# Bias projection of an attention block: one product of 512 tokens, or four of 128 tokens in TensorE's column groups

## The reference

```python
v  = (xn @ v_w + v_b)                                  # 16 heads of 16
qm = (xn @ qmod_w + qmod_b)   # [tokens, 16 heads]     the query's bias per head
km = (xn @ kmod_w + kmod_b)   # [tokens, 16 heads]     the key's bias per head
qc, kc = xn @ cq_w, xn @ ck_w                          # 16 heads of 8
scores = kernel[i - j] + qm[i] + km[j] + 0.15 * qc[i] @ kc[j] / sqrt(8)   # causal
attn = softmax(scores); out = LN(h + FFN(h)), h = LN(xn + attn @ v @ out_w + out_b)
gate = silu(FP4-quantised gated FFN of xn);  y = x + out * gate
```

## Time and profile before

| | |
|---|---|
| median of 3 runs | 1970.54 us (1969.98 to 1972.34) |
| profiled execution | 1971.34 us, of which the span of the trace 1969.5 us |
| mean granted TensorE clock | 0.98 of full |
| TensorE (PE) busy | 93% of the span |
| DVE / POOL / ACT busy | 81% / 56% / 46% |
| DMA | mean 84 GB/s |

### The profile page before, as it was taken

The page is one execution under the profiler, slowest core; times in us unless marked ns, Lnnn a source line. Parts: engine busy times, 40 slices in busy tenths (PEclk is TensorE's granted clock), DMA queues, the critical chain, the costliest instruction groups (busy, mean ns, idle before and its releaser), DMA issues.

```text
span 1969.5 us, 41524 instructions
## 1 busy us (share of the span) xinstructions
PE 1841.2 (93%) x12508; PEld 1309.0 (66%) x12508; DVE 1598.7 (81%) x5214; ACT 900.4 (46%) x1816; POOL 1102.8 (56%) x788
## 2 busy tenths in 40 slices
PE   9578899999999999999999999999999999999986
PEld 3134667676776767676776767676676767677765
DVE  6969978888888978888887978888897888888762
ACT  1115454454535454454645554453645444453532
POOL 3424747464655746564665746565664746465471
PEclk9769999999999999999999999999999999999998
DMA  4523223232322323232223323232222322232110
GB/s 138 174 93 89 63 75 117 73 88 69 105 64 82 88 73 106 73 95 73 85 64 99 89 73 106 62 95 83 76 74 73 116 73 88 70 106 67 40 65 22
DMA packets 129154, 165.44 MB, mean 84 GB/s; under 512 B 9821, under 2 KB 90718, under 8 KB 129028
## 3 DMA queue, kind: packets, MB, share of 16 engines
q1 hardware_dynamic: 129034, 164.29, 28.6%
HBM read 127.85 MB, written 36.41 MB: 83 GB/s over the span
## 4 chain that ended last, share of the span: by engine, by line
PE 59%; DVE 20%; issue 14%; ACT 3%; DMA 1%; DVEq 1%; POOL 1%; SPq 1%; ACTq 0%; POOLq 0%
PE ps L738 11%; PE ps L729 11%; PE ps L679 8%; PE ps L696 4%; PE ps L579 4%; PE ps L602 3%; PE ps L636 3%; DVE nmax L994 3%; PE ps L711 3%; PE ps L589 3%; PE ps L652 2%; PE ps L632 2%; DVE ps L994 2%; DVE st L916 2%; DVE slot L1061 1%
## 5 line engine op out<-in xcount | busy, mean ns | idle before, releaser
L1132 POOL TENSOR_TENSOR Pr<-Pr,Tz 128x768 f32<-128x768 f32 (+2 forms) x384 | 477.9, 1273 | 243.7 <-ACT Pr L802 242.7
L994 DVE CUSTOM_DVE_ANT_0 ps<-ps,future 128x512 f32<-128x512 f32 (+3 forms) x1024 | 474.9, 517 | 52.7 <-issue 52.4
L802 ACT ACTIVATE Pr<-ps 128x384 f32<-128x384 f32 x512 | 243.0, 489 | 370.0 <-PE ps L636 367.1
L729 PE MATMUL ps<-catT,w 128*128 128x256 f32 x1024 | 237.3, 380 | 0.7 <-ACT catT L867 0.7
L602 PE MATMUL ps<-KS,QS 108*128 108x512 bf16 (+3 forms) x1024 | 217.2, 303 | 21.0 <-DVE nmax L994 14.7
L738 PE MATMUL ps<-w,gT 128*128 128x256 f32 x1024 | 233.0, 381 | 0.9 <-ACT gT L878 0.9
L791 ACT ACTIVATE ps<-ps 128x512 f32<-128x512 f32 x256 | 150.5, 588 | 132.4 <-PE ps L632 130.2
L1024 DVE SCALAR_TENSOR_TENSOR Pr<-ps,Tz 128x512 f32<-128x512 f32 x256 | 175.0, 684 | 41.3 <-ACT ps L791 37.9
L738 PEld LDWEIGHTS ps<-w,gT 128*128 128x128 f32 x1024 | 190.9, 190 | 25.8 <-ACT gT L878 1.3
L729 PEld LDWEIGHTS ps<-catT,w 128*128 128x128 f32 x1024 | 189.7, 190 | 26.7 <-ACT catT L867 1.0
L696 PE MATMUL ps<-wdT,hqT 128*128 128x256 f32 x768 | 178.2, 381 | 0.7 <-ACT hqT L843 0.7
(11 more groups left out here) (213 smaller groups left out, 3247.9 us busy)
## 6 DMA issues: line engine op xcount, KB each, us to landing
Tz<-kernel_rows SPq DMA_DIRECT2D x128, 512.0 KB, 3.8
KS<-k_parts SPq DMA_DIRECT2D x32, 384.0 KB
QS<-q_parts SPq DMA_DIRECT2D x64, 192.0 KB
hY<-in_x SPq DMA_DIRECT2D x20, 512.0 KB, 4.8
xn<-in_x SPq DMA_DIRECT2D x16, 512.0 KB, 3.6
out<-y SPq DMA_DIRECT2D x16, 512.0 KB, 3.0
q_parts<-q_sp SPq DMA_DIRECT2D x16, 384.0 KB, 3.3
k_parts<-k_sp SPq DMA_DIRECT2D x16, 384.0 KB, 2.4
```

Source lines behind the costliest of these rows:

```text
L729: ins = mm(dst[:, i * n:(i + 1) * n], w1[:, c, f * P:(f + 1) * P], catT[:, c, hf * n:(hf + 1) * n], start=c == 0, stop=c == KD - 1)
L802: inc(af(Pr[:, p % 4, e, at:at + wd], src[:, 0:wd], ACT.Exp), "a_exp")
L994: ins = v.tensor_tensor_reduce(o, o, future[:, S - n:S], -1.0, 3e38, ALU.add, ALU.min, nmax[:, 2 * pl + e, it:it + 1])
L1132: ins = g.tensor_tensor(a, a, Tz[:, p % 2, :, P * j:P * j + PAST[j]], ALU.mult)
```

## The change

`proj.2` is issued as four products for each of the two chunks, one for each tile of 128 tokens. The product of tile t writes partitions 32t to 32t+31 of the bank (128 columns of it), so it stands in the t-th group of 32 columns of TensorE. `bias_sp` and `bias_r` now have 128 partitions (tile, then query and key heads) and 128 tokens. ACT, DVE and POOL work on these shapes with the same number of instructions; the bias column `bb` is loaded four times (eight tiny transfers at the start for two). `splitio` writes the bias parts with eight transfers of 16 partitions x 3 parts x 128 tokens for two of 16 x 3 x 512. Nothing in the order of the steps changes.

```diff
-        bb = sb("bb", [2 * H, 1])
+        bb = sb("bb", [P, 1])
-        bias_sp = sb("bias_sp", [2 * H, 3, S], BF16)
-        q_r, k_r, bias_r = sb("q_r", [P, S]), sb("k_r", [P, S]), sb("bias_r", [2 * H, S])
+        bias_sp = sb("bias_sp", [P, 3, P], BF16)
+        q_r, k_r, bias_r = sb("q_r", [P, S]), sb("k_r", [P, S]), sb("bias_r", [P, P])
-        d_split = event("d_split", 8, 16)
+        d_split = event("d_split", 6 + 2 * T, 16)
...
-                    sp.dma_start(qb_d[:, 3:6, :], bias_sp[0:H]).then_inc(d_split.sem, 16)
-                    sp.dma_start(kb_d[:, 0:3, :], bias_sp[H:2 * H]).then_inc(d_split.sem, 16)
+                    for t in range(T):
+                        cols, r = slice(t * P, (t + 1) * P), 2 * H * t
+                        sp.dma_start(qb_d[:, 3:6, cols], bias_sp[r:r + H]).then_inc(d_split.sem, 16)
+                        sp.dma_start(kb_d[:, 0:3, cols], bias_sp[r + H:r + 2 * H]).then_inc(d_split.sem, 16)
...
-                        ins = mm(dst[0:wt.shape[2], :], wt[:, c, :], xnT[:, c, :], start=c == 0, stop=c == KD - 1)
+                        if s[1] < 2:
+                            ins = mm(dst, wt[:, c, :], xnT[:, c, :], start=c == 0, stop=c == KD - 1)
+                            continue
+                        for t in range(T):
+                            ins = mm(dst[2 * H * t:2 * H * (t + 1), 0:P], wt[:, c, :], xnT[:, c, t * P:(t + 1) * P],
+                                     start=c == 0, stop=c == KD - 1)
...
-                        ins = af(sp_[:, 0, :], src[0:2 * H, :], ACT.Identity, bias=bb[:, 0:1])
+                        ins = af(sp_[:, 0, :], src[:, 0:P], ACT.Identity, bias=bb[:, 0:1])
...
-                        ins = v.scalar_tensor_tensor(r[:], src[0:2 * H, :], bb[:, 0:1], sp_[:, 0, :], ALU.add, ALU.subtract)
+                        ins = v.scalar_tensor_tensor(r[:], src[:, 0:P], bb[:, 0:1], sp_[:, 0, :], ALU.add, ALU.subtract)
...
-                    (bw[:, :, H:2 * H], chunks("kmod_w")), (bb[0:H, :], column("qmod_b")), (bb[H:2 * H, :], column("kmod_b"))],
+                    (bw[:, :, H:2 * H], chunks("kmod_w")), *[(bb[H * (2 * t + i):H * (2 * t + i + 1), :], column(n)) for t in range(T) for i, n in enumerate(("qmod_b", "kmod_b"))]],
```

## The result

| | before | after |
|---|---|---|
| median (range) | 1971.4 us of 6 runs (1970.0 to 1974.4) | 1957.5 us of 6 runs (1956.5 to 1958.9) |
| ratio after / before | | 0.9928, 95% interval 0.9917 to 0.9939 |
| profiled execution, its span | 1971.34, 1969.5 us | 1956.46, 1954.7 us |
| one turn of the loop | 111.91 to 111.94 us | 110.63 to 111.32 us |

A forecast was written before the change was run, and what follows sets the result against it. No engine bounds the whole kernel: TensorE leads the bias stretch, DVE only 0.38 us behind. Per turn 1.25-0.77+0.1 = 0.6 us, times 14 is 8.4, plus 0.45 head: 8.9 us less, 1961.6; range 1951 to 1972.

The forecast's parts named there:

- rival 1: In the loop, the later `T.5` costs nothing and TensorE's gain is all kept: 18 us less, 1952.6; chance 0.25.
- TensorE's block: Bias projection in each turn: 16 passes in 0.53 us for 1.78, a gain of 1.25 us (0.88 to 1.34).
- Evictions: Bias evictions on 128 columns: DVE's residual 0.28 us, gaining 0.45; POOL's low part 0.4 us, gaining 0.75.
- SP: SP's queue: eight bias issues 0.45 us apart, 3.6 us in all; `T.5` issued at 871.1, landing at 875.7.
- DVE's wait: At `muld.5.0` in each turn: due at 874.3, DVE waits 1.4 us for `T.5`.
- What of the wait is given back: Ahead of `mx.0.0.0`: of 1.4 us waited DVE has 0.63 to spare, so 0.77 us a turn is lost.
- The 0.1 us for a shifted order: Small DVE operations stretched beside POOL: counted as 0.1 us gained a turn, bounded by 0.3 either way.
- Head: Prologue, at DVE's bias residual: 0.45 us gained once; six more tiny bias loads counted as nothing, 1 us at most.
- Rival 2: SP's longer issues, 0.61 us each, become the bound: 0.8 us lost a turn, 1981 us; chance 0.10.
- Rival 3: TensorE's four column groups don't run side by side: block 2.2 us, 0.9 lost a turn, 1983 us; chance 0.03.
- Rival 4: In the loop, gain and loss cancel (issue pitch 0.48 to 0.53 or block 0.9 us): 1969 us; chance 0.17.

The follow-up runs named there:

- with `T.5` first: Changed kernel with the kernel-row load `T.5` issued ahead of the eight bias transfers in the loop: 1954.9 us (0.9903), in a later series 1958.2 us (0.9923).
- the run in one group: Kernel before with its bias product cut into the same 16 passes, all in one column group: 1970.4 us in one run.
- the run with `mul.4` reversed: Changed kernel with the three instructions of POOL's `mul.4` issued in reverse order: 1964.3 us in one run, beside 1967.5 for before.

## Why the prediction was right, and where it was not

The direction held, and so did TensorE's gain, the later `T.5` and DVE's wait for it; what the wait costs did not. The gain was 14.0 us for 8.9 forecast, inside the range. The range, drawn wide enough to hold rival 1 too, would have held it with either account of the wait, so the time alone confirms neither. Step by step:

- *TensorE's block*: 0.57 us for 0.53 forecast. PV's pace carried over to the wider weights: both start four passes within 20 ns, and the next four 109 ns after them (133 once in the bias block), so 27 ns a pass. `mx.0.0.0` moved from +35.57 to +34.31, 1.26 us for 1.25.
- *Evictions*: residual 0.34 us for 0.28, low part 0.43 for 0.40.
- *SP*: 0.47 us from one issue to the next for 0.45; `T.5` 0.72 us behind the eighth issue's start, as after the second one before. It stands at +21.89; the forecast's 871.1 is +22.14, and the difference is that the low part ended 2.14 us earlier after the mark, not 1.9. The landing was taken as 4.6 us from one turn; it is 4.0 to 4.8 us before (median 4.5) and 4.1 to 5.1 after (median 4.6), so it did not change much, but it scatters, and that decides which turns are long.
- *DVE's wait*: 1.17 us in the mean for 1.4 forecast, present in all 14 turns. Nearly all of the difference is that `T.5` is 0.25 us earlier; DVE asked for it at +25.35, where the forecast's 874.3 is +25.34.
- *What of the wait is given back* is the term that failed. The prediction took 0.63 us of spare time and charged the rest, 0.77 us in every turn. Measured: 0.65 us in four turns of 14, nothing in the others. The prediction named this itself as a sign of being wrong (more than 0.63 us to spare), and the sign came. The step of the prediction that failed is "of that wait DVE has 0.63 to spare": from `muld.5.0` to `mx.0.0.0` it took DVE's work as of fixed length. It isn't. The two small scalings together take 1.03 us without a wait (0.30+0.73, with `T.5` first), 0.61 with a wait of 1.03 us, 0.37 with 1.32 (0.18+0.19) and 0.97 with 1.34 (0.79+0.18). With the idle time of 0.44 us, 0.18 us that the next `muld` waited for ACT without the wait, and the 0.66 us of stretching that goes away, up to 1.28 us are absorbed, not 0.63; then 0.6 us of stretching come back at once.
- *The 0.1 us for a shifted order* was the place where this stood in the sum, bounded by 0.3 either way. The bound was too narrow (up to 0.66 us won, 0.60 lost again), and it was treated as independent of the wait.
- *Head*: 0.45 us expected once; it can't be seen in a stretch that scatters by 5 us from trace to trace.

In numbers: 1.27 less 4x0.65/13 is 1.07 us a turn for the forecast's 0.6, and 13 intervals of this are the 13.96 us. The rest of the profiled difference (14.8 us of span) is -3.9 ahead of the first mark and +3.1 behind the last, both within the scatter of equal kernels.

Rival 1 (`T.5` costs nothing, 1952.6) is what ten turns of 14 do, but not by its reason: `T.5` is late in all of them. The time measured, 1957.5, lies between it and the forecast. Rival 2 (longer issues) would have needed over 0.51 us from one issue to the next; it was 0.47, though the run with before's product and eight transfers, 13.5 us slower than before, shows that its mechanism is there. That the earlier low part is what keeps it from deciding was not run by itself. Rival 3 (not side by side) fell with the 0.57 us, and the run in one group shows the 1.86 us that it was about. By the Trainium skill, page TensorE: Matmul & The Clock Gate, section Part 3 (What overlaps and what doesn't), weight loads overlap running products only where row groups differ (the text above that list also lets a load into the background weight buffer be pulled ahead, and no trace here shows into which buffer a load went); neither block here agrees with the list, the one of four column groups (16 loads and passes in 0.57 us) nor the one in a single group, where 1.86/16 = 0.116 us a pass leaves next to nothing for a load beside the 0.111 of streaming. Rival 4 (gain and loss cancel) would have needed a cost of 1.0 to 1.3 us in every turn.

For the stretched operations the Trainium skill has a rule, on the page SBUF — State Buffer, in the list below its diagram: VectorE and GpSimd share one pair of ports; of a GpSimd instruction and a VectorE one that is in a 2-port mode, or has two inputs in SBUF while GpSimd reads SBUF, the one that starts first holds the pair for its whole instruction, and the other is blocked. The ends of L898 with the ends of POOL's instructions, and the run with `mul.4` reversed, agree with it; which mode L898 runs in, no trace shows. The reciprocal between the two scalings (L900) always takes 0.43 us, beside POOL or not, so not every small operation is stretched; the rule leaves room for that.

Left open: why the first part of the kernel scatters, and whether the version with `T.5` first is faster than the change by the 1.1 to 2.5 us of its loop; the runs so far are too few for that. The gain in the 14th turn can't be read from mark to mark, and is not in the 13.96 us.

## What to carry to other kernels

A product with few output columns is cheap to spread over TensorE's column groups by tiles of tokens: it also gives evictions that use all partitions. Count what the new layout does to the transfers, and look at which load is queued behind them; here six more issues of 0.47 us alone pushed it back by 2.8 us, which cost 0.87 us a turn; in the change the earlier end of POOL's low part and shorter DVE operations beside POOL took up most of that. When DVE and POOL work side by side, the cost of a delay can be a staircase: before a spare time is written into a sum, look at which small DVE operations end exactly with an instruction of POOL, and where they would fall after the shift.

## What the runs showed of the hardware that was not expected

- A scaling of 128x44 float32 on DVE takes 0.19 us alone, and when it is stretched beside POOL it ends 0.04 us behind an instruction of POOL: 0.30, 0.42, 0.73, 0.79 or 0.95 us in the rows shown. A delay of 0.02 us (waits of 1.32 and 1.34) moved the start of `mx.0.0.0` by 0.6 us. A reciprocal of the same size took 0.43 us every time.
- A product of DVE of 128x704 that began 0.03 us after a multiplication of POOL took 2.54 us in place of 0.89.
- Sixteen float32 passes of 128 columns with their weight loads: 0.57 us in four column groups, 1.86 us in one, all with 128 rows.
- Issuing a transfer of 16 partitions in 48 runs of 256 bytes holds SP for 0.42 us (0.47 from one to the next), and it lands after 1.5 us (median; 5.5 at most).
- The same six passes in the prologue took 5.49 us in five executions and 2.8 to 3.1 in seven, with a granted clock of 1.00 listed for all; the loop started 289.4 to 290.8 us in with the slow ones and 285.3 to 288.3 with the fast ones.
